# Two elementwise jobs of the first stage move from VectorE to GpSimd

## The reference, cut to what matters

```
xn = (x - mean) / sqrt(var + eps)                  # layernorm of x
x1 = xn @ L0_gnn_W1 + L0_gnn_b1                    # the embedding, 1250 x 512
x  = x + concat([x1, gnn_out], 1) + mix(xn)        # the residual
W[row, col] += edge_weight                         # 20000 edges (src, dst), a scatter used in layer 1
counts[dst, src] += 1                              # the same edges, for the graph layer
```

## Time and profile before

| | us |
|---|---|
| median of 3 runs | 2344.4 |
| the profiled execution | 2347.38, its span 2345.7 |
| TensorE busy, share of the span | 2186.8, 93% |
| VectorE busy | 1513.4, 65% |
| GpSimd busy | 254.5, 11% |
| mean granted TensorE clock | 0.958 |
| the changed stage | 0 to about 127 us of the span |

### The profile page before, as it was taken

One profiled execution on the slowest core, in us unless ns is written; L12 is line 12 of the kernel. 1 busy time (PEld: TensorE's weight loads), 2 busy tenths in 40 slices (PEclk: granted clock), 3 DMA queues, 4 the chain that ended last, 5 costly groups with the idle time before them and its releaser, 6 DMA issues. The chain is left out here.

```text
span 2345.7 us, 29203 instructions
## 1 busy us (share of the span) xinstructions
PE 2186.8 (93%) x10522; PEld 1803.9 (77%) x10522; DVE 1513.4 (65%) x2245; ACT 1015.1 (43%) x1515; POOL 254.5 (11%) x253
## 2 busy tenths in 40 slices
PE   7999999979969999976999999969999999989998
PEld 5778888867857778775888888857778888878786
DVE  8735474568858788866999999966733343345422
ACT  4134243338725544526888888851022122121120
POOL 0067774000010000020000000011000000000000
PEclk9999999988989999967999999989999999999999
DMA  5431231114448535164555554136420120134224
GB/s 189 152 103 36 50 83 24 65 65 146 145 151 312 224 152 224 52 235 152 189 201 185 207 184 177 63 120 202 133 76 34 48 81 32 56 104 152 75 86 153
DMA packets 114121, 299.89 MB, mean 128 GB/s; under 512 B 18802, under 2 KB 42218, under 8 KB 113974
## 3 DMA queue, kind: packets, MB, share of 16 engines
q1 hardware_dynamic: 103094, 276.52, 33.9%
q0 software_dynamic: 10880, 21.48, 3.3%
HBM read 295.24 MB, written 124.16 MB: 179 GB/s over the span
## 5 line engine op out<-in xcount | busy, mean ns | idle before, releaser
L2723 DVE TENSOR_TENSOR ex_wl<-exlast,ex_wh 128x1024 fp32r<-128x1024 f32 x216 | 252.7, 1219 | 9.0 <-ACT ex_wh L2790 8.4
L2790 ACT ACTIVATE ex_wh<-exlast 128x1024 fp32r<-128x1024 f32 x216 | 217.5, 1058 | 17.8 <-PE ex_pu L2746 8.8
L1273 POOL DMA_INDIRECT scratch_slots<-packed x160 | 198.2, 1239 | 56.7 <-issue 56.7
L324 PE MATMUL ps<-kept,xh 128*128 128x512 f32 (+2 forms) x480 | 163.2, 427 | 7.8 <-DVE xl L3014 5.0
L2123 PE MATMUL gl_bank<-gl_gh,gl_al 125*125 125x512 f32 x385 | 153.3, 398 | 9.7 <-DVE gl_al L2338 9.7
L1570 PE MATMUL ps<-kept,xl 128*128 128x512 f32 (+1 forms) x640 | 159.6, 391 | 0.0
L1572 PE MATMUL ps<-kept,xh 128*128 128x512 f32 (+1 forms) x640 | 158.3, 389 | 0.0
L1576 PE MATMUL ps<-kept,xh 128*128 128x512 f32 (+1 forms) x640 | 158.2, 389 | 0.0
L2125 PE MATMUL gl_bank<-gl_gh,gl_ah 125*125 125x512 f32 x385 | 152.8, 397 | 0.0
L2124 PE MATMUL gl_bank<-gl_gl,gl_ah 125*125 125x512 f32 x385 | 152.6, 396 | 0.0
L1572 PEld LDWEIGHTS ps<-kept,xh 128*128 128x128 f32 (+1 forms) x640 | 118.5, 185 | 26.9
(11 more groups left out here) (513 smaller groups left out, 4892.2 us busy)
## 6 DMA issues: line engine op xcount, KB each, us to landing
exlast<-in_experts SPq DMA_DIRECT2D x216, 512.0 KB
exfirst<-in_experts SPq DMA_DIRECT2D x112, 512.0 KB, 6.3
scratch_seats<-raw SPq DMA_DIRECT2D x95, 512.0 KB
raw<-in_qkv SPq DMA_DIRECT2D x48, 512.0 KB, 6.7
xr<-scratch_res SPq DMA_DIRECT2D x27, 512.0 KB, 4.3
xr<-scratch_seats SPq DMA_DIRECT2D x27, 512.0 KB, 3.6
scratch_res<-xr SPq DMA_DIRECT2D x25, 512.0 KB, 3.9
raw<-in_wo SPq DMA_DIRECT2D x16, 512.0 KB, 3.4
```

Source lines behind the costliest of these rows:

```text
L324: i = e.matmul(o, a, b[:, cut], start=first and n == 0, stop=final and n == 2)
L1273: e.indirect_dma_start(dram["slot_rows"], bass.IndirectOffsetOnAxis(idx[:, k:k + 1].bitcast(U32), 0), pay[:, k, :], None).then_inc(scat.se ...
L2723: return e.tensor_tensor(wl[:, n % RING], raw[unit[1]], wh[:, n % RING].bitcast(F32), ALU.subtract)
L2790: e.activation(wh[:, n % RING], raw[unit[1]], ACT.Copy).then_inc(high.sem)
```

## The change

GpSimd gets, after its constants, a loop over the chunks: pick(2c), pick(2c+1), then the residual's add(c). VectorE loses these 9 picks and 10 adds and the drain ahead of each add; it waits before the evict of chunk c for the add of chunk c-2, which reads the same x1 buffer, and gets one drain at chunk 9. The picks wait now for the one-hot's signal too. Nothing else moves.

```
@@ def gpsimd
+            def add(c):
+                r = rows_of(c)
+                t = slot(c)[0:r, 0:NH]
+                e.wait_ge(*evicted[c])
+                e.tensor_tensor(t, t, x1_of(c)[0:r], ALU.add).then_inc(summed.sem)
+
+            def pick(i):
+                e.wait_ge(*hot_done[i])
+                e.wait_ge(*local[last(i)])
+                o = loc(i)[0:EP, 0:wide(i)]
+                e.tensor_tensor(o, o, hot[:, i % HR, 0:wide(i)], ALU.mult).then_inc(picked.sem)
+
+            for c in C:
+                for i in range(2 * c, min(2 * c + 2, NP)):
+                    pick(i)
+                add(c)
@@ def vector
-            def pick(i):
-                e.wait_ge(*local[last(i)])
-                o = loc(i)[0:EP, 0:wide(i)]
-                e.tensor_tensor(o, o, hot[:, i % HR, 0:wide(i)], ALU.mult).then_inc(picked.sem)
...
                 if c == 9:
                     e.wait_ge(*gathered[QS[-1]])
+                    d()
...
                 if c >= 2:
                     e.wait_ge(*x1_out[b][c - 2])
+                    e.wait_ge(*summed[c - 2])
...
                 e.tensor_tensor(x1_of(c)[0:r], py[b][0:r], bias[0:r], ALU.add).then_inc(evicted.sem)
-                e.drain()
-                t = slot(c)[0:r, 0:NH]
-                e.tensor_tensor(t, t, x1_of(c)[0:r], ALU.add).then_inc(summed.sem)
...
                 if c + 3 < TC:
                     moments_of(c + 3)
-                for i in range(2 * c, min(2 * c + 2, NP)):
-                    pick(i)
                 for i in range(2 * c + 3, min(2 * c + 5, NP)):
                     make_hot(i)
```

## The result

The changed kernel takes 2354.7 us in the median of its five runs (2352.8 to 2361.7), where the kernel before has 2344.4: +10.3 us, a ratio of 1.005 with an interval of 1.003 to 1.0071. It is slower by half a percent, and the interval stays clear of 1. The forecast was 2359.5 with a range of 2342.5 to 2371.

What follows compares the result with a forecast made beforehand. TensorE was taken as the bound in chunks 1 to 3, VectorE close behind and the bound in three later waits. 6.4 + 0.7 + 6.5 + 0.7 + 0.4 + 2.4 - 2.0 = +15.1 us: 2359.5 us, range 2342.5 to 2371.

Steps and rivals of the forecast that it cites:

- chunk 0: First stage: pick(0) holds a one-hot, then pick(1) holds the scale, moving TensorE's transposes from 28.02 to 34.4: +6.4 us.
- chunk 1: First stage: pick(2) overlaps the end of the scale by more than the slack holds: +0.7 us.
- chunk 2: First stage: pick(3) holds a one-hot, pick(4) and pick(5) hold the scale, so evict(2) comes late: +6.5 us.
- chunk 3: First stage: one more brush of a scale against a pick, mostly hidden by TensorE's own time: +0.7 us.
- chunks 4 and 5: First stage: one scale-against-pick brush in chunk 4, +0.4 us; from chunk 5 on GpSimd has only adds, which don't collide.
- clock: TensorE at about half speed after each of two 6 us idle times in chunks 0 and 2: +1.2 each, +2.4 us.
- gains, and the rest behind: Adds and drains off VectorE shorten three TensorE waits, before gathers, last transposes and the query: together -2.0 us.
- The price of a pick: GpSimd's two-input pick of 1920 elements: 4.3 us, from 2.2 ns per element, two reads and one write.
- The mirror: SBUF sharing: a reading GpSimd instruction holds VectorE's two-SBUF-input instructions and the normalisation L272 until it ends.
- Rival A: Engines don't hold each other up, or a pick costs under 3 us: only -2.0 left, 2342.4 us; chance 0.23.
- Rival B: GpSimd becomes the pace, with holding but lucky order, last pick ending at 81.7: +5.9, 2350.3 us; chance 0.20.
- Rival C: VectorE loses every race, each of chunks 0 to 3 costing 6.5 us: +28.8, 2373.2 us; chance 0.12.

Runs made afterwards that it cites:

- two comparisons: The changed kernel, unedited, measured twice against the kernel before: 2354.7 us (ratio 1.005), and again 2355.3 us (ratio 1.004).
- race won: First profile of the changed kernel, where chunk 0's scale began before pick(1): 2352.8 us, next stage at 132.1 against 128.10 before.
- race lost: Unedited changed kernel, profiled twice more, the scale held by pick(1) in chunk 0: 2356.2 and 2349.4 us, next stage at 137.59 and 138.23.
- the first two profiles: Two profiles of the changed kernel, nothing edited between them: 2352.8 and 2356.2 us.
- the third: Third profile of the changed kernel, not edited: one run of 2349.4 us, next stage at 138.23.
- the two of before: Two profiles of the kernel before, unaltered: 2347.4 us and 2340.4 us.
- the second: Second profile of the changed kernel, not edited: 2356.2 us, next stage at 137.59; median of that measurement 2355.3 us, ratio 1.004.

## Why the prediction was right, step by step

It named the mechanism and the sign: +15.1 forecast, +10.3 and +11.3 measured in two comparisons. That the number fell in its range is partly luck. The range reaches from no change at all to +27, the two large terms of the sum are off by up to 5.6 us each, and no profile shows the stage that the forecast described. Terms against what the marks of the two kinds of profile show (race won, race lost):

```
term                              forecast    won    lost
chunk 0                             +6.4      +0.8   +4.5
chunk 1                             +0.7      +1.1   +1.1
chunk 2                             +6.5      +1.1   +1.1
chunk 3                             +0.7      +0.7   +0.7
chunks 4 and 5                      +0.4      +0.75  +1.0
clock                               +2.4       0     +1.3
gains, and the rest behind          -2.0      -0.5   -0.3
sum at the next stage              +15.1      +4.0   +9.5
```

*The price of a pick*: 3.84 us alone, 4.25 to 4.31 where it starts while a one-hot or the scale of VectorE still runs; forecast 4.3. For 1920 elements 3.84 is 2.0 ns each, and the forecast's 2.2 from one read and one write was near enough. The Trainium skill (GPSIMD Engine Reference, "Performance versus the Vector engine") led to an estimated 4.2; the measured 3.84 is 9% less.

*The mirror*: right. A reading GpSimd instruction holds VectorE's two-input instructions until its own end, even at one element (L266 0.21 to 2.67, L270 0.16 to 3.39), and the scale (0.81 to 4.35). Rival A is refuted.

*Chunk 0*: right in kind where the race is lost (both holds are where they were put, +4.5 and +5.1 instead of +6.4), and far too dear where it is won (+0.8: the one-hot's hold alone). I had the one-hot end at 28.5 and pick(1) ahead of the whole scale. In the first two profiles the one-hot ended at 27.3 and 27.45, since pick(0) began at 22.45 and 22.60 and not at 23.1, and took 3.85 and not 4.3; in the third pick(0) began at 23.51 and the one-hot ended at 28.4, nearly as forecast. The ranks of piece 0 wander by a microsecond from profile to profile. So the scale's instructions and pick(1) are ready within some tenths of a microsecond of each other, which I had not seen: I took for certain what is a race.

*Chunk 2*: this term failed, +6.5 against +1.1. I let VectorE lose the scale twice in a row there, from a shift of 6.4 to 7.1 us carried through. In all three profiles of the change, lost races in chunk 0 among them, L272 of chunks 1 to 3 slips through (0.81 us each time), and each chunk has one hold on the path: the pick of a chunk's first piece against L266. (A jump of this size, 6.75, did come in chunk 2 with the picks alone on GpSimd, by another way: a held add of VectorE, which the change doesn't have.) What replaces it is a cadence, 11.96 us instead of 10.85 in chunks 1 and 2: 1.1 a chunk and no jump. The forecast's chunk 0 and 2 together came to 12.9, the profiles' to 6.2 at most (the third).

*The clock*: right where the idle time exists. After 5.16 us idle chunk 1 took 1.3 us more than in the profile with the race won, against +1.2 for each stretch. There was one such stretch there, not two, and none in the first chunks with the race won.

*The gains*: the step is right and the sum not. From the evict to the moments it takes 0.60 us (100.97 to 101.57) instead of 1.39, so the 0.8 is there. What it brought can't be read from TensorE's wait before the last transposes: 1.28 in this profile, with the clock at 1.00 behind it, but 0.30 and 1.52 in the other two of the change, and 2.65 and 1.83 in the two of before. Evict 7 waits for the keys anyway, and came 12.5 us behind evict 6 instead of 12.2. The wait of 1.35 before L178 is gone in this profile (in the second it is 1.25), and one of 1.75 stands before a matmul at 117.38, for VectorE's split. There the add of chunk 7 had held a two-input instruction of 160 elements, 1.49 us instead of 0.46, and behind this wait the matmuls ran at 0.62 us, at a granted clock of 0.86 from 113 to 125. The cast that the gathers wait for took 1.32 us beside an add instead of 0.33, and TensorE's wait there rose from 0.49 to 1.23. VectorE's rows and TensorE's after:

```profile
86.97 1.32 DVE L800 CAST em_packs<-em_excl 100x320 bf16<-100x320 f32 x1
...
114.62 1.49 DVE L811 SCALAR_TENSOR_TENSOR packed<-em_fhd,em_fd 125x160 f32<-125x160 f32 x1
```

```profile
88.34 5.29 PE L552 MATMUL ps<-em_packs,raw 100*125 100x4 bf16 x64 [1.23 <-DVE em_packs L800]
...
117.38 0.50 PE L324 MATMUL ps<-kept,xh 128*98 128x512 f32 x1 [1.75 <-DVE xl L661]
```

I had priced the adds' holds at nothing, since I had looked only at the moments, which are not held. The cast has one input in SBUF, as the scale has: the forecast's list of what can be held was short of it.

*Rival B* (GpSimd the pace) had a number as near as the forecast's, 2350.3, and something of the truth: GpSimd is 89% busy in the windows of chunks 1 and 2. But its picks wait for ScalarE's takes in each chunk, and the last one ends at 71.2 us with the race won and 76.2 with it lost, not at the 81.7 of this rival. So its throughput isn't the bound; its latency is, inside the loop. *Rival C* (6.5 us in each of chunks 0 to 3) is out as well: in the three profiles no chunk behind the first costs more than 2.9 us.

## What to carry to other kernels

Before moving work from VectorE to GpSimd, list what VectorE runs beside it: each instruction with two inputs in SBUF, however small, and each scale or cast may wait as long as the moved instruction lasts. Such a move costs nothing only where the moved instruction fits into the slack of what it holds (2.0 to 2.5 us did here, 3.84 did not); it pays only where VectorE is what the others wait for, and no variant here gained anything that can be measured. The shares of busy time tell neither. Where two ready times lie within some tenths of a microsecond, give both outcomes with a chance each; and if a semaphore decides the order, it has to decide every instance.

## What was not expected

- One program with two courses: who comes first, a pick or a scale (28.12 and 28.13 in one profile, 28.20 and 27.98 in another), decides 3.7 us in one chunk and 1.3 in the next.
- GpSimd's writes alone, 4.4 us of memsets for each piece, cost the kernel nothing (0.9995), while multiplies of 3.4 to 3.8 us at the same moments cost 21.7 us (1.0089).
- Held time counts as busy: VectorE shows 11.5 us busy in a chunk for less work than what took 9.8 before.
